# Selective scan on one core: five of sixteen C products moved to a third path

## The reference, cut to what matters

```python
# per image: K=4 directions, L=2304 positions, 384 channels d, N=16 states n
dA = exp(d_t[..., None] * A)
h  = h * dA + (d_t * u_t)[..., None] * B_t[:, :, None, :]
y  = einsum('bkdn,bkn->bkd', h, C_t)      # sum over the 16 states of h[n] * C[n]
```

## Time and profile before

| | |
|---|---|
| Median of 3 runs | 16809.22 us (16805.1 to 16815.5) |
| The profiled execution's own time | 16797.47 us |
| Its span | 16795.7 us |
| Busy, share of the span | DVE 81%, PE 76%, POOL 69%, ACT 61% |
| Mean granted PE clock | 0.928 |

### The profile page before, as it was taken

The page is one execution under the profiler, slowest core; times in us unless marked ns, Lnnn a source line. Parts: engine busy times, 40 slices in busy tenths (PEclk is TensorE's granted clock), DMA queues, the critical chain, the costliest instruction groups (busy, mean ns, idle before and its releaser), DMA issues.

```text
span 16795.7 us, 194014 instructions
## 1 busy us (share of the span) xinstructions
PE 12714.0 (76%) x40364; PEld 6215.0 (37%) x40364; DVE 13568.4 (81%) x14264; ACT 10234.9 (61%) x19950; POOL 11552.8 (69%) x4612
## 2 busy tenths in 40 slices
PE   5777877778777797777977779677796777967779
PEld 2333433334333343333433334333343333433334
DVE  8998579985799857998579984899848998489984
ACT  4666566655666556665566655666556665566655
POOL 6998069970699707996079960899608996089950
PEclk8999999999999999999999999999999999989999
DMA  2332023320233202332023320233203332033310
GB/s 85 105 104 88 5 81 106 104 84 5 85 106 106 78 5 88 106 106 74 5 92 106 106 70 5 96 106 107 65 5 101 105 106 63 5 103 106 106 59 9
DMA packets 822107, 1276.73 MB, mean 76 GB/s; under 512 B 27488, under 2 KB 814560, under 8 KB 815136
## 3 DMA queue, kind: packets, MB, share of 16 engines
q1 hardware_dynamic: 820960, 1264.99, 23.6%
HBM read 1241.29 MB, written 23.59 MB: 75 GB/s over the span
## 4 chain that ended last, share of the span: by engine, by line
POOL 29%; PE 27%; issue 24%; DVE 15%; ACT 2%; DVEq 1%; POOLq 1%; ACTq 0%; SPq 0%; DMA 0%
POOL area L1229 19%; DVE area L794 11%; POOL area L1239 8%; PE ps L648 8%; PE ps L659 8%; PE ps L492 3%; DVE area L813 2%; PE ps L443 1%; PE ps L465 1%; PE ps L545 1%; PE ps L534 1%; DVE area L777 1%; POOL area L1218 1%; PE ps L560 1%; DVE area L304 1%
## 5 line engine op out<-in xcount | busy, mean ns | idle before, releaser
L492 PE MATMUL ps<-area,ident 128*128 128x384 f32 x18432 | 7309.7, 542 | 3428.8 <-POOL area L1239 1639.5
L794 DVE TENSOR_TENSOR_SCAN area<-ps,hst,area 128x384 f32<-128x384 f32 x9216 | 8628.9, 1002 | 467.3 <-ACT ps L1038 403.1
L1229 POOL TENSOR_TENSOR area<-area 128x1152 f32<-128x1152 f32 x3072 | 7996.8, 2636 | 32.1 <-POOL area L1218 32.1
L1038 ACT ACTIVATE ps<-area,a_neg 128x384 f32<-128x384 f32 x9216 | 5238.0, 580 | 2487.8 <-DVE area L794 2468.1
L492 PEld LDWEIGHTS ps<-area,ident 128*128 128x128 f32 x18432 | 3620.7, 207 | 7235.9 <-POOL area L1239 2315.2
L1239 POOL TENSOR_TENSOR area<-area 128x1152 f32<-128x1152 f32 x1152 | 3030.4, 2631 | 89.7 <-ACT hst L1006 87.8
L813 DVE TENSOR_TENSOR area<-area,ps 128x1152 f32<-128x1152 f32 x1920 | 2560.6, 1334 | 5.2 <-ACT ps L1016 5.2
L1163 ACT ACTIVATE area<-ps,t_neg,area 128x768 f32<-128x768 f32 x1728 | 1619.1, 987 | 925.2 <-PE ps L648 925.2
L1197 POOL TENSOR_TENSOR area<-w_in,ones 96x256 f32<-96x256 f32 x27 | 34.6, 1282 | 2054.8 <-DVE area L304 1351.1
L648 PE MATMUL ps<-area 64*128 64x384 f32 x6912 | 1370.3, 515 | 64.0 <-ACT area L1163 53.4
L659 PE MATMUL ps<-area 128*64 128x384 f32 x6912 | 1342.5, 501 | 0.0
(11 more groups left out here) (115 smaller groups left out, 8206.5 us busy)
## 6 DMA issues: line engine op xcount, KB each, us to landing
area<-bc_rows SPq DMA_DIRECT2D x1536, 768.0 KB, 6.3
area<-in_x SPq DMA_DIRECT2D x17, 1728.0 KB, 9.7
out<-area SPq DMA_DIRECT2D x8, 1728.0 KB, 8.8
bc_rows<-area SPq DMA_DIRECT2D x16, 576.0 KB, 4.9
w_dt<-in_w_dt SPq DMA_DIRECT2D x1, 768.0 KB, 6.4
w_in<-in_w_in SPq DMA_DIRECT2D x1, 576.0 KB, 4.7
w_qkv<-in_w_qkv SPq DMA_DIRECT2D x1, 576.0 KB, 5.3
w_xp<-in_w_xp SPq DMA_DIRECT2D x1, 384.0 KB, 5.0
```

What stands on the lines that cost most here:

```text
L492: m = e.matmul(ps[:, 5 + j, 0:CH], ident[:], prod[:, j], start=i == 0, stop=i == N - 1)
L794: e.tensor_tensor_scan(rev(hb[:, i % NH, j], k), rev(ps[:, 2 + j, 0:CH], k), rev(dbu[:, i % NH, j], k), hst[:, i, j:j + 1], ALU.mult, ALU. ...
L1038: e.activation(ps[:, 2 + j, 0:CH], dlt[:, par, j], ACT.Exp, scale=a_neg[:, j, k, i:i + 1]).then_inc(da, 1)
L1229: e.tensor_tensor(dbu[:, i % NH], du[:, par], row_b[:, q % 2, i % ROWS:i % ROWS + 1].broadcast_to([128, J, CH]), ALU.mult).then_inc(dbus, 1)
```

## The change

The 16 states are dealt out anew: POOL_N has 4 states (0, 3, 8, 12), DVE_N has 7 (2, 5, 6, 9, 11, 14, 15) and five, TURN_N = (1, 4, 7, 10, 13), take a third path. For such a state n, positions are taken in three blocks tt of 128, one in each of the slots n+1, n+2, n+3 (the third block of state 13 falls in slot 0 of the next chunk):

1. PE, `turn`: three transposes of 128 x 128 put the block of the three channel tiles into bank 0, positions on partitions.
2. ACT, `turned_product`: one activation Copy 128 x 384 from bank 0 to the SBUF tile `ht`, with C at each position as the per-partition scale (`c_t`).
3. PE, `turned_sum`: three matmuls with `ht` as weights and the identity moving (128 columns) add the block, turned back, to banks 5 to 7. It stands one slot after its transposes.

`c_t` is made at the start of each image's scan stage: 36 transposes of `stage` blocks by PE into banks 5, 6, 7, 0, 1 in five groups, copied by ten small DVE copies. ACT waits for these (`ct_cp`) before its first softplus. Bank 0 now serves the turned blocks, the next chunk's delta tiles and the `ln` results, with waits between them. DVE's `times_c` works in place in `hb` (`hc` is gone), so a DVE state's buffer is freed by its sum. The sums of states are issued by PE at slots given by SUM_AT. The softplus steps, delta tiles and additions are put at other slots.

```diff
+POOL_N = (0, 3, 8, 12)
+TURN_N = (1, 4, 7, 10, 13)
+SUM_AT = {0: 3, 2: 4, 3: 6, 5: 7, 6: 8, 8: 11, 9: 12, 11: 13, 12: 15, 14: 16, 15: 17}
+ADD_AT = {5: 0, 9: 1, 10: 2}
+LN_AT = {6: 0, 7: 1, 10: 2}
...
+                def turn(g, m):
+                    n, at, tt = turn_at(m)
+                    if tt == 0:
+                        e.wait_ge(scan, g * 48 + (3 + 3 * n + 3))
+                    e.wait_ge(turn_cp, g * NT + (NT + at))
+                    for j in range(J):
+                        i = e.matmul(ps[:, 0, j * 128:(j + 1) * 128], hb[:, n % NH, j, tt * 128:(tt + 1) * 128],
+                                     ident[:], is_transpose=True)
+                    i.then_inc(turn_mm, 1)
+                def turned_sum(g, m):
+                    n, at, tt = turn_at(m)
+                    e.wait_ge(turn_cp, g * NT + (NT + at + 1))
+                    for j in range(J):
+                        i = e.matmul(ps[:, 5 + j, tt * 128:(tt + 1) * 128], ht[:, tt, j * 128:(j + 1) * 128], ident[:],
+                                     start=False, stop=False)
+                    i.then_inc(turn_sum, 1)
...
+                    for m in range(N):
+                        if m == 0 and last:
+                            turn(g - 1, N)
+                        if nxt and m in (2, 3):
+                            e.wait_ge(dp_rd, g3 + (3 + m))
+                        if nxt and m - 1 in LN_AT:
+                            e.wait_ge(dp_v, g3 + (3 + LN_AT[m - 1] + 1))
+                        if turn_at(m):
+                            turn(g, m)
+                        if m < 2 and last:
+                            slot_end(g - 1, N + m)
+                        if SUM_AT[0] == m:
+                            state_sum(g, 0)
+                        if turn_at(m - 1):
+                            turned_sum(g, m - 1)
+                        for i in SUM_ORDER[1:]:
+                            if SUM_AT[i] == m:
+                                state_sum(g, i)
+                        if nxt and m < 3:
...
+                            delta_tile(*nxt, m)
...
-                        if (i - NH) % N in POOL_N:
-                            e.wait_ge(ysum, g16 + (N + i - NH + 1))
+                        free, before = (i - NH) % N, i < NH
+                        if free in TURN_N:
+                            e.wait_ge(turn_mm, g * NT + ((NT, 0)[before] + 3 * TURN_N.index(free) + 3))
+                        else:
+                            e.wait_ge(ysum, g * NS + ((NS, 0)[before] + SUM_ORDER.index(free) + 1))
...
-                    e.tensor_tensor(hc[:, d % 2], hb[:, i % NH], ps[:, 1:2, 0:CH].broadcast_to([128, J, CH]),
+                    e.tensor_tensor(hb[:, i % NH], hb[:, i % NH], ps[:, 1:2, 0:CH].broadcast_to([128, J, CH]),
...
+                when = {1: (("x", 0),), 2: (("x", 1),), 3: (("x", 2), ("abs", 0)), 4: (("abs", 1), ("exp", 0)),
+                        5: (("abs", 2), ("exp", 1)), 6: (("exp", 2), ("ln", 0)), 7: (("ln", 1),), 10: (("ln", 2),)}
...
+                def turned_product(g, k, c, m):
+                    n, at, tt = turn_at(m)
+                    t = c * 3 if k < 2 else (NC - 1) * 3 - c * 3
+                    e.wait_ge(turn_mm, g * NT + (NT + at + 1))
+                    e.wait_ge(turn_sum, g * NT + (NT + at - 2))
+                    e.activation(ht[:, tt], ps[:, 0, 0:CH], ACT.Copy,
+                                 scale=c_t[:, ds(t + (k % 2 * MT + tt), 1), k // 2 * N + n]).then_inc(turn_cp, 1)
```

More of the change, by code:

```diff
@@ L56 @@
 NH = 4
-DEL, DU, HC, DBU, HB = (XS + i * JC for i in (0, 2, 4, 6, 10))
+DEL, DU, DBU, HB = (XS + i * JC for i in (0, 2, 4, 8))
 SCAN_END = HB + NH * JC
 STG = Y
-POOL_N = (1, 4, 6, 9, 12, 14)
-DVE_N = tuple(i for i in range(N) if i not in POOL_N)
-NP, ND = len(POOL_N), len(DVE_N)
+HT = SCAN_END
+CT_T = HT + JC
+POOL_N = (0, 3, 8, 12)
+TURN_N = (1, 4, 7, 10, 13)
+DVE_N = tuple(i for i in range(N) if i not in POOL_N + TURN_N)
+NP, ND, NT = len(POOL_N), len(DVE_N), 3 * len(TURN_N)
+SUM_AT = {0: 3, 2: 4, 3: 6, 5: 7, 6: 8, 8: 11, 9: 12, 11: 13, 12: 15, 14: 16, 15: 17}
+SUM_ORDER = tuple(sorted(SUM_AT, key=SUM_AT.get))
+NS = len(SUM_ORDER)
+ADD_AT = {5: 0, 9: 1, 10: 2}
+LN_AT = {6: 0, 7: 1, 10: 2}
+GM = 5
 Z = J * L
@@ L211, in build @@
         ysum = sem("ysum")
+        ct_mm = sem("ct_mm")
+        ct_cp = sem("ct_cp")
+        turn_mm = sem("turn_mm")
+        turn_cp = sem("turn_cp")
+        turn_sum = sem("turn_sum")
         yev = sem("yev")
@@ L342, in rev, with turn_at, ct_group @@
             return ap if k < 2 else ap[:, ::-1]
-        ps3 = ps[:, 2:5, 0:CH]
+        def turn_at(m):
+            for t, n in enumerate(TURN_N):
+                if n + 1 <= m <= n + 3:
+                    return n, 3 * t + m - n - 1, m - n - 1
+            return None
+        def ct_group(q):
+            return min(8, 2 * MT - 8 * q), (5, 6, 7, 0, 1)[q]
         def y_chunk(k, c):
@@ L476, in scan_phase @@
                     delta_tile(0, 0, j, 2 + j)
+                for q in range(GM):
+                    n, bank = ct_group(q)
+                    for i in range(n):
+                        o, t = divmod(8 * q + i, MT)
+                        m = e.matmul(ps[:, bank, 64 * i:64 * i + 64], stage[:, o, t * 128:(t + 1) * 128],
+                                     ident[0:4 * N, 0:4 * N], is_transpose=True)
+                    m.then_inc(ct_mm, 1)
+                e.wait_ge(ct_cp, b * GM + GM)
@@ new lines, in turned_sum, with state_sum @@
+                def turned_sum(g, m):
[5 more added lines that the diff above has]
+                    i.then_inc(turn_sum, 1)
+                def state_sum(g, i):
+                    if i in POOL_N:
+                        e.wait_ge(hcp, g * NP + (NP + POOL_N.index(i) + 1))
+                    else:
+                        e.wait_ge(hcs, g * ND + (1 + DVE_N.index(i) + 1))
+                    if i == 0:
+                        e.wait_ge(yev, g + 1)
+                    for j in range(J):
+                        m = e.matmul(ps[:, 5 + j, 0:CH], ident[:], hb[:, i % NH, j], start=i == 0, stop=i == N - 1)
+                    m.then_inc(ysum, 1)
@@ L478, in body, with slot_end @@
+                def slot_end(g, m):
+                    if turn_at(m - 1):
+                        turned_sum(g, m - 1)
+                    for i in SUM_ORDER:
+                        if SUM_AT[i] == m:
+                            state_sum(g, i)
                 def body(k, c, par, last, nxt):
                     g = e.snap(b * 24 + (c + k * NC))
[L480 to L496, removed]
-                                e.wait_ge(dp_v, g3 + 3)
-                            delta_tile(*nxt, i // 2)
-                        if i in (8, 10, 12):
-                            j = (i - 8) // 2
@@ L507, in scan_phase @@
                 walk(e, body)
+                g = e.snap(b * 24 + 23)
+                turn(g, N)
+                slot_end(g, N)
+                slot_end(g, N + 1)
             def back(b):
@@ L714, in _ @@
             e.tensor_scalar(a_neg[:], a_neg[:], -1.0, None, ALU.mult).then_inc(prepared, 1)
-            for s, v in ((xp_dv, 2), (scan, 3), (hcs, 1), (yev, 1), (cen, 2), (x1s, 4), (x2s, 4), (nrm, 6), (stored, 16)):
+            for s, v in ((xp_dv, 2), (scan, 3), (hcs, 1), (yev, 1), (cen, 2), (x1s, 4), (x2s, 4), (nrm, 6), (stored, 16),
+                         (turn_mm, NT), (turn_cp, NT), (turn_sum, NT)):
                 e.sem_inc(s, v)
@@ L778, in delta @@
                                            op0=ALU.max, op1=ALU.add).then_inc(dp_v, 1)
+                for q in range(GM):
+                    n, bank = ct_group(q)
+                    e.wait_ge(ct_mm, b * GM + (q + 1))
+                    for a in range(2):
+                        m = e.tensor_copy(c_t[:, 8 * q:8 * q + n, N * a:N * a + N],
+                                          ps[:, bank, 0:64 * n].rearrange("p (t r) -> p t r", r=4 * N)
+                                          [:, :, 2 * N * a + N:2 * N * a + 2 * N])
+                    m.then_inc(ct_cp, 1)
                 for j in range(J):
@@ L1008, in c_copy @@
                 def c_copy(g, i):
-                    if i in POOL_N:
+                    if i not in DVE_N:
                         return
@@ L1039, in body @@
                                          scale=a_neg[:, j, k, i:i + 1]).then_inc(da, 1)
+                        todo = when.get(i, ()) if nxt else ()
+                        for op, j in todo:
+                            if op == "x":
+                                softplus(g + 1, 1 - par, nxt[0], op, j)
                         if i == 0 and last:
@@ L1042, in body @@
                             c_copy(g - 1, N - 1)
+                            turned_product(g - 1, *last, N)
                         if i >= 1:
@@ L1045, in body @@
                             c_copy(g, i - 1)
+                        if turn_at(i):
+                            turned_product(g, k, c, i)
```

(20 more changed lines are left out.)

38 lines of the change are left out of this document (25 added, 13 removed).

## The result

The changed kernel takes 16,986.5 us (median of 4 runs, 16,975.4 to 16,995.8) against 16,807.4 (4 runs): ratio 1.0105, 95% interval 1.0088 to 1.0123. It is 1% slower, where 3.5% faster was forecast. The profiled execution took 16,975.4 us.

A forecast was written before the change was run, and what follows sets the result against it. POOL sets the pace at 59.7 us per chunk, DVE close behind; afterwards DVE's 53.9 plus 2.4 of stalls gives 56.3. Saving 591 us from 16797.5 gives 16,206, plus 12 for the median: 16,220 us, range 15,960 to 16,780.

The forecast's parts named there:

- POOL and DVE lose the work, at the prices given: Per chunk, POOL drops two C products, 59.7 to 54.5 us; DVE drops three, 57.7 to 53.9 us.
- Prices on PE: Turned-sum instructions taken at 0.12 us each, bounds 0.113 and 0.22; PE 41.5 us per chunk, 51 at the upper bound.
- loads of about 0.265 us: PE weight loads said to stand inside six matmuls taking 2.20 us, as evidence that load and pass overlap.
- The clock: the step that failed: PE's half-clock pieces follow idle stretches of some 4 us, which get shorter; 0.2 us of DVE stall per chunk.
- rival 2: PE's clock stays low at 1.2 GHz, a chunk asks PE for 80 us and PE bounds: 20,700 us; chance 0.03.
- What PE's order holds up: PE's in-order queue makes sums late: scan 4 stalls 0.15 us at slot 3, scan 12 0.35 at slot 11.
- ACT's slot 2: Scaled copy, x step, hold and store_y take ACT 3.2 to 3.3 us there; DVE stalls 1.6 to 1.7 us.
- Once per image: 36 transposes at each image's scan-stage start delay ACT's softplus by 5.3 us, 9.6 at half clock; 7 taken.
- The sum: DVE stalls 2.4 us, chunk 56.3, 3.4 less than before; 591 us saved over eight images, median 16,220 us.
- Rival 1: Scaled copies wait for in-order PE, delaying Exps: chunk 63.1, 17,520 us; decides from 5.5 us of stalls; chance 0.11 slower, 0.05 unchanged.

The follow-up runs named there:

- e1: Changed kernel plus useless PE matmuls, nine ahead of slot 3's wait and eight ahead of slot 11's: 16,522 us, ratio 0.9828 to the kernel before.
- e2: Changed kernel with only PE's order changed, sum 0 ahead of slot 3's wait and sum 8 at slot 10: 16,436 us, ratio 0.9781.
- e6: Changed kernel with e2's PE order, store_y ahead of slot 2's scaled copy, and thirteen useless PE matmuls in slot 2: 16,185 us, ratio 0.9621.
- e10: Kernel before plus nine useless PE matmuls ahead of each of the six sums per chunk that wait for POOL: 16,760 us, ratio 0.9966.

## Why the prediction was wrong, point by point

- **POOL and DVE lose the work, at the prices given.** Right. POOL's products are at 2.63 us, DVE's product at 1.33, the scan at 0.995. POOL has gaps now.
- **Prices on PE.** Right. Six turned-sum instructions take 0.67 us from start to start (5037.84 - 5037.17), 0.11 each; transposes 0.32 to 0.38 for three: the lower bound and not the upper. The Trainium skill ("TensorE: Matmul & The Clock Gate", Part 3) has a weight load overlap a matmul only in another row group. With load and pass one after the other this would be 0.22 each; the trace disagrees. The forecast's "loads of about 0.265 us" were misread: they are a merged piece of 1.59 us divided by six. The page of the kernel before has 207 ns for one load of this line, and since the six start every 0.32 us, they do stand inside the passes.
- **The clock: the step that failed.** I wrote that half-clock pieces follow idle stretches of some 4 us, that these get shorter, and left 0.2 us per chunk. PE's mean clock is 0.92 in the middle, before 0.93. The length of the pauses was the wrong thing to read. The trace of the kernel before already had twelve instructions at 5.83 us rather than 4.03 behind a pause of 2.19 us:

```profile
5066.93 4.03 PE L492 MATMUL ps<-area,ident 128*128 128x384 f32 x12
...
5083.83 5.83 PE L492 MATMUL ps<-area,ident 128*128 128x384 f32 x12 [2.19 <-POOL area L1239]
```

  What counts is the work behind the pause: rival 2 looked at a clock that stays low and gave it 3 in 100, and no rival priced the mixture, a sum at 4.2 us rather than 2.2 in the two slots where I had found no margin. Those rows were at hand: up to 2 us more in slots 3 and 11. The runs showed some 2.8 us per chunk of DVE's waiting in place of the 0.2 (next point).
- **What PE's order holds up.** The places were right, slots 3 and 11 and no others; the size was not. Stalls for PE: forecast 0.15 + 0.35, measured 714.6 / 192 = 3.7 us per chunk. With the clock up (e1) they are 179.2 / 192 = 0.93. So of the 3.2 us missed 2.8 are the clock's, and 0.4 my estimate of the slots. That 0.4 is all slot 11's: in e1 scan 4 waits 35 / 192 = 0.18 us (forecast 0.15) and scan 12 144 / 192 = 0.75 (forecast 0.35). The split is by removing the clock first. PE's order, changed alone, removes all of these waits (e2), so most of the loss needs both: a slow sum, and a sum that is due when made.
- **ACT's slot 2.** Forecast 1.7 us, measured 451.1 / 192 = 2.35 for all Exp waits. In the slot shown ACT waited 0.98 us for the transposes (forecast 0.6) and held store_y for 1.9 (forecast 1.6).
- **A term that was missing.** In the changed kernel ACT stands still for 2.1 to 5.0 us in 28 of the 192 chunks, waiting for nothing that the profile shows, 92.8 us in all, ahead of a first Exp; the kernel before has no such wait on this line. It comes only in the fourth chunk of a direction, where the program jumps back to the head of the loop over chunks. In e6 it comes there every time (32 times, 140.7 us), and the long chunks of its steady middle are 59.7 to 60.9 us.

```profile
ACT ps L1143 <- issue: 92.8, 28, 5.0
```

  The program became longer (244,473 instructions, before 194,014, and 400 packets of one instruction queue, before 286), so that code loading at the jump is a likely cause; no run tested it. e10, with 235,486 instructions of which the added ones are PE's, has such a wait only 4 times (18.4 us), so the length of the whole program alone doesn't set it.
- **Once per image.** Forecast 7 us, measured 3.9: the softplus starts 5.22 us after the first delta tile, before 1.31. The 36 transposes have 64 x 64 outputs and took 2.44 us, where the forecast priced them as 128 x 128, 4.3 us.

```profile
4364.01 2.17 PE L496 MATMUL ps<-area,w_dt 128*128 128x384 f32 x6 [0.99 <-DVEq L288]
4366.11 2.44 PE L505 MATMUL ps<-ident,area 64*128 64x64 f32 x36
...
4369.23 1.52 ACT L1080 ACTIVATE area<-ps,b_dt 128x384 f32<-128x384 f32 x3 [3.90 <-DVE area L870]
```

- **The sum.** Forecast DVE waits of 2.4 per chunk against 6.3 in the trace ((1259.7 - 48.5) / 192; the 48.5 for POOL were there before): 3.9 x 192 = 750 us, and 16,206 + 750 = 16,956, near the 16,975 of the profiled execution. Nothing large is left over: the 3.9 us are 3.0 of PE (3.7 against 0.7), 0.65 of Exp (2.35 against 1.7), and the rest mostly waits of slot 0 for ACT.
- **Rival 1** (PE in order holds back ACT) came out on the right side and decides at the point that I gave, 5.5 us of stalls per chunk: the trace has 6.3. But its mechanism is the smaller part. ACT does wait, 1615.1 / 2880 = 0.56 us for each scaled copy, as it would; more than half of what DVE waits for is PE's sums themselves (714.6 of 1259.7 us).

## What to carry to other kernels

When an engine gets new work in program order, list the places where its result is due with no margin, and price each of them at the slow level of its clock if a pause stands ahead of it, as a bound: here one place was slow nearly always and the other in under half of the chunks. An average clock or busy share doesn't show this: 0.93 and 0.92 here hide a loss of 464 us in one kernel and of 62 in the other. The mend is cheap: a sum moved into the pause ahead of it (e2), or useless matmuls in it (e1), turned 1% slower into 2.2 and 1.7% faster; the new order with `store_y` moved and matmuls in slot 2 made it 3.8% faster (e6). Useless matmuls that another engine has to wait for cost something themselves, 79 us in e1.

## What the runs showed of the hardware

- The length of one pause of PE didn't tell which clock the work behind it got. In slot 11 of the changed kernel the pauses are 1.5 to 3.5 us long both ahead of the 89 slow sums and ahead of the 103 others, 2.8 us on average in both groups. A pause of 2.19 us was followed by a sum of 3.68 us, one of 2.18 in the next chunk by a sum of 2.10.
- Transposes and turned sums run at 0.11 to 0.13 us per instruction at full clock, and a dense stretch of them, with sums between, stays at 1.00 (5026.90 to 5034.50 above).
- A chunk's length in the changed kernel scatters by 7 us from one to the next, though each does the same work (58.2 to 65.1 us). With PE's work in slots 3 and 11 at full clock (e1) it is 57.1 to 62.7, and in e6 55.8 to 56.2 but for the fourth chunk of each direction; the kernel before, with POOL as its bound, has 59.6 to 59.8 in 18 of 20.
